# Moving the first pass's statistics, masks, normalising and residual add off VectorE onto ScalarE, TensorE and GpSimd

## The reference

```
x = x + L0(gn(x))      # a 2-D selective scan ("Mamba" block)
x = x + L1(gn(x))      # attention with 12 heads and relative positions

L0:  xh, z = split(x @ in_proj.T)                  # 192 channels each
     u = silu(depthwise_conv3x3(xh) + conv_b)
     four directions k (row and column order, each forward and backward):
       dt, B, C = split(x_proj[k] @ u)             # 24, 16, 16 rows
       dt = softplus(dt_proj[k] @ dt + dt_b[k])
       h[n] = h[n] * exp(dt * A[n]) + dt * u * B[n]    # over the tokens, n = 0..15
       y += sum_n h[n] * C[n] + D[k] * u
     y = layernorm(y) * g + b;  return (y * silu(z)) @ out_proj.T
```

## Time and profile before

| | |
|---|---|
| median of 3 runs | 3307.79 us (3305.24 to 3314.67) |
| the profiled execution | 3309.41 us, span 3307.6 us |
| TensorE busy | 2748.0 us (83% of the span) |
| VectorE busy | 2366.0 us (72%) |
| ScalarE busy | 1557.4 us (47%) |
| GpSimd busy | 1335.6 us (40%) |
| mean granted TensorE clock | 0.948 |

### The profile page before, as it was taken

How to read it: one execution, slowest core, us unless ns; L and a number is a source line. 1 busy time by engine, 2 the same in 40 slices (tenths; PEclk the granted TensorE clock), 3 DMA queues, 4 the chain that set the end, 5 groups by cost and what they waited for, 6 DMA issues and landing times. The chain is left out here.

```text
span 3307.6 us, 40573 instructions
## 1 busy us (share of the span) xinstructions
PE 2748.0 (83%) x15824; PEld 1382.7 (42%) x15824; DVE 2366.0 (72%) x2262; ACT 1557.4 (47%) x1908; POOL 1335.6 (40%) x636
## 2 busy tenths in 40 slices
PE   3577777887678876777667999989998999989999
PEld 1222223332233332222222665556554665555655
DVE  1598899999999999999982466625664356625665
ACT  4445644555435564444431356514563346514564
POOL 4478766887668876766651100011000200011000
PEclk8789998999999999999896999999999999999999
DMA  1334443355443544445541111020111110020110
GB/s 61 128 115 133 153 144 141 130 140 159 145 149 127 140 159 145 161 134 144 182 137 60 30 33 52 1 71 1 33 52 40 33 33 25 29 71 1 33 52 20
DMA packets 93429, 297.51 MB, mean 90 GB/s; under 512 B 15804, under 2 KB 18504, under 8 KB 93224
## 3 DMA queue, kind: packets, MB, share of 16 engines
q1 hardware_dynamic: 93224, 294.73, 28.6%
HBM read 238.57 MB, written 23.07 MB: 79 GB/s over the span
## 5 line engine op out<-in xcount | busy, mean ns | idle before, releaser
L1608 POOL TENSOR_TENSOR arena<-arena 128x1024 f32<-128x1024 f32 x384 | 902.9, 2365 | 325.9 <-DVE arena L1092 277.3
L1092 DVE TENSOR_TENSOR_SCAN arena<-PS,arena 128x1024 f32<-128x1024 f32 x384 | 878.2, 2287 | 86.1 <-ACT PS L1445 62.5
L1445 ACT ACTIVATE PS<-arena,a_inf,a_neg 128x1024 f32<-128x1024 f32 x384 | 463.8, 1208 | 776.8 <-DVE arena L1092 772.4
L564 PE MATMUL PS<-arena,ident 128*128 128x512 f32 x1568 | 804.1, 639 | 19.3 <-ACT arena L1456 15.1
L1225 DVE CUSTOM_DVE_ANT_1 arena<-PS,arena 128x1024 f32<-128x1024 f32 x384 | 467.6, 1219 | 350.4 <-PE PS L851 350.4
L1533 ACT ACTIVATE arena<-arena,neg_max 128x1024 f32<-128x1024 f32 x384 | 441.0, 1149 | 513.4 <-DVE neg_max L1225 513.4
L555 PE MATMUL PS<-arena,sel 96*128 96x512 bf16 x768 | 247.7, 406 | 413.0 <-DVE arena L1100 409.3
L1100 DVE TENSOR_TENSOR arena<-arena,PS 128x1024 f32<-128x1024 f32 x384 | 459.3, 1196 | 9.7 <-PE PS L555 8.9
L564 PEld LDWEIGHTS PS<-arena,ident 128*128 128x128 f32 x1568 | 318.5, 204 | 304.2 <-issue 246.9
L851 PE MATMUL PS<-arena 64*128 64x512 f32 x1536 | 433.1, 641 | 11.1 <-DMA arena<-arena 11.1
L862 PE MATMUL PS<-ident,arena 128*128 128x128 f32 x3072 | 413.9, 278 | 2.6 <-ACT arena L1533 2.6
(11 more groups left out here) (125 smaller groups left out, 2286.2 us busy)
## 6 DMA issues: line engine op xcount, KB each, us to landing
arena<-b_rows SPq DMA_DIRECT2D x256, 512.0 KB, 3.7
arena<-b_rows SPq DMA_DIRECT2D x256, 256.0 KB, 4.0
arena<-arena SPq DMA_DIRECT2D x192, 128.0 KB, 2.9
arena<-arena SPq DMA_DIRECT2D x120, 64.0 KB, 2.0
normed<-xn SPq DMA_DIRECT2D x5, 1536.0 KB, 6.4
normed<-x_in SPq DMA_DIRECT2D x4, 1536.0 KB, 7.9
residual<-x_in SPq DMA_DIRECT2D x4, 1536.0 KB, 8.0
x<-residual SPq DMA_DIRECT2D x4, 1536.0 KB, 6.4
```

The lines of the kernel that those rows point to most:

```text
L564: last = pe.matmul(dst[:, half(h)], lhs, rhs[:, half(h)], start=start, stop=stop, skip_group_check=True)
L1092: dve.tensor_tensor_scan(HS[:, at % 2, ::step], DA[:, ::step], DBU[:, at % R3, ::step], 0.0, ALU.mult, ALU.add).then_inc(scan_done.sem, 1)
L1445: act.activation(DA, DELTA[:, tile % 2, :], ACT.Exp, bias=a_inf[:, col:col + 1], scale=a_neg[:, col:col + 1]).then_inc(da_ready.sem, 1)
L1608: pool.tensor_tensor(DBU[:, at % R3, :], DU[:, tile % 2, :], BSB[:, at % R3, :], ALU.mult).then_inc(dbu_ready.sem, 1)
```

## The change

- **Statistics.** ScalarE makes the sums of both group norms: Copy and Square with an accumulator, over 1024 columns for the first norm, over the 512 of each output half for the second. It reads the group means from PSUM (`group_means`), GpSimd makes variance and bias, ScalarE rstd and the normalising (Identity with scale and bias).
- **x + out** is a third product, an identity times x, in TensorE's output product; ScalarE copies the sum out.
- **The mask** of the softplus is a Relu on ScalarE into uint8 (item 8); the scaling by 1/3 is folded into the square.
- **The split of C**: GpSimd subtracts (from a copy in SBUF), ScalarE casts.
- **Image 0's front**: its additions, caps and gates go from GpSimd to VectorE.
- **Positions**: a front's group norm moves to the end of the image before (negative positions; for image 1 squeezed into items 0 to 3), the tap additions are spaced otherwise, and many jobs stand elsewhere.

VectorE keeps scan, product with C, series and choice, and centring and scaling of the layernorm. The core of the diff:

```diff
+EARLY = 20
-PE_FRONT = {("stats",): 4, ("xh", 0): 12, ("xh", 1): 13, ("xh", 2): 14, ("pad", 0): 36, ("pad", 1): 37, ("pad", 2): 38,
+PE_FRONT = {("stats",): -8, ("xh", 0): 5, ("xh", 1): 6, ("xh", 2): 7, ("pad", 0): 25.5, ("pad", 1): 26, ("pad", 2): 27,
             ("z", 0, 0): 56, ("z", 0, 1): 57, ("z", 0, 2): 58, ("z", 1, 0): 61, ("z", 1, 1): 62, ("z", 1, 2): 63,
             ("dts", 0): 70, ("dts", 1): 71, ("dts", 2): 72, ("bc", 0): 75, ("bc", 1): 76, ("bc", 2): 77}
+PE_MID = {("y", 0, 0): 9, ("y", 0, 1): 10, ("y", 0, 2): 11, ("y", 1, 0): 13, ("y", 1, 1): 14, ("mean", 0): 21,
+          ("mean", 1): 22, ("var", 0): 30, ("var", 1): 31, ("out", 0): 43, ("out", 1): 44, ("out", 2): 45,
+          ("out", 3): 46, ("out", 4): 47, ("out", 5): 48, ("stats",): 53}
-ACT_FRONT = {("rstd",): 8, ("xh",): 16, ("pad",): 40, ("z", 0): 60, ("z", 1): 64.5,
...
+ACT_FRONT = {("stat", 0, 0): -20, ("stat", 0, 1): -19, ("stat", 1, 0): -18, ("stat", 1, 1): -15, ("stat", 2, 0): -14,
+             ("stat", 2, 1): -11, ("means",): -6, ("rstd",): -4, ("norm", 0): -3, ("norm", 1): -2, ("norm", 2): -1,
+             ("xh",): 8, ("pad",): 28, ("z", 0): 59.5, ("z", 1): 64.5,
+             ("sig", 0, 0): 35, ("sig", 0, 1): 38, ("sig", 0, 2): 40, ("sig", 1, 0): 62, ("sig", 1, 1): 65,
+             ("sig", 1, 2): 65.5, ("sig", 2, 0): 60, ("sig", 2, 1): 64, ("sig", 2, 2): 67.5, ("sig", 3, 0): 70,
+             ("sig", 3, 1): 74, ("sig", 3, 2): 75, ("ucopy", 0): 49.5, ("ucopy", 1): 50, ("ucopy", 2): 67,
+             ("ucopy", 3): 69, ("dts",): 73.5, ("brows",): 79, ("bchi",): 80, ("bmid",): 83, ("blo",): 86}
+ACT_MID = {("yf", 0): 12, ("yf", 1): 16, ("sq", 0): 27, ("sq", 1): 28.5, ("rstd",): 33, ("affine", 0): 35.5,
+           ("affine", 1): 37, ("out", 0): 43.9, ("out", 1): 44.9, ("out", 2): 45.9, ("out", 3): 46.9, ("out", 4): 47.9,
+           ("out", 5): 48.9, ("means",): 54.9, ("rstd2",): 56, ("norm", 0): 58.9, ("norm", 1): 60.5, ("norm", 2): 61}
+POOL_FRONT = {("var",): -5.5, ("bias",): -3.5, ("cap", 0): 36.5, ("u", 0): 42, ("cap", 2): 63, ("cap", 1): 64,
+              ("u", 1): 65.9, ("gate", 0): 68.5, ("cap", 3): 71.5, ("gate", 1): 77, ("rest", 0): 81.5, ("rest", 1): 85}
+POOL_MID = {("gate", 0): 38.5, ("gate", 1): 40, ("sums",): 50, ("var",): 55.5, ("bias",): 57}
...
-SP_FRONT = {("next_x",): 72, ("z_store",): 79, ("b_store",): 83, ("bcs",): 87}
+SP_FRONT = {("next_x",): 72, ("z_store",): 80, ("b_store",): 83, ("bcs",): 89}
...
+            if f == 1 and at < 0:
+                item = (at + EARLY) * 0.2
...
                     half_product(banks(k % 2, 1), h, [
                         (W["w_out"][:, 0, c * P:(c + 1) * P], flat(yf(m, 0))),
-                        (W["w_out"][0:XT, 1, c * P:(c + 1) * P], flat(yf(m, 1)[0:XT, :]))]).then_inc(op_psum.sem, 1)
+                        (W["w_out"][0:XT, 1, c * P:(c + 1) * P], flat(yf(m, 1)[0:XT, :])),
+                        (idn, flat(X[:, c, :]))]).then_inc(op_psum.sem, 1)
...
             def soft_series(tile):
 
-                dve.wait_ge(soft_e.sem, soft_e.at(tile + 1))
-                dve.tensor_scalar(MASK, SE, SMALL, None, ALU.is_lt)
                 dve.wait_ge(soft_q2.sem, soft_q2.at(tile + 1))
-                dve.scalar_tensor_tensor(out=SQ3, in0=SQ3, scalar=2.4375, in1=SE, op0=ALU.add,
+                dve.scalar_tensor_tensor(out=SQ3, in0=SQ3, scalar=0.8125, in1=SE, op0=ALU.add,
                                          op1=ALU.mult).then_inc(soft_q.sem, 1)
...
+                elif what == "out":
+                    k, = args
+                    h, c = divmod(k, CT)
+                    act.wait_ge(op_psum.sem, op_psum.at(2 * CT * m + k + 1))
+                    act.activation(X[:, c, half(h)], banks(k % 2, 1), ACT.Copy, accum_out=half_sums[:, h, c, 0:1])
+                    act.activation(banks(k % 2, 1), banks(k % 2, 1), ACT.Square, scale=1.0 / IMG,
+                                   accum_out=half_sums[:, h, c, 1:2]).then_inc(x_saved.sem, 1)
...
+            def small_mask(tile):
+
+                act.activation(MASK, SE, ACT.Relu, bias=mask_top[:, 0:1], scale=-MASK_TOP / SMALL
+                               ).then_inc(soft_mask.sem, 1)
```

More of the change, by code:

```diff
@@ L49 @@
[L49 to L53, removed]
@@ L73, in due @@
-def due(table, i):
-    return sorted((job for job, at in table.items() if i <= at < i + 1), key=table.get)
+            POOL_FRONT[("add", _m, _j)] = _b
+SIG_ORDER = sorted(range(4), key=lambda which: ACT_FRONT[("sig", which, 0)])
+SIG_DONE = sorted(range(4), key=lambda which: ACT_FRONT[("sig", which, 2)])
+CAP_ORDER = sorted(range(4), key=lambda which: POOL_FRONT[("cap", which)])
+SP_FRONT = {("next_x",): 72, ("z_store",): 80, ("b_store",): 83, ("bcs",): 89}
+SP_MID = {("x_load",): 1, ("z_load",): 2, ("x1_store",): 52, ("xn2_store",): 67}
@@ L78, in in_order, with front_due, mid_due @@
 def in_order(table):
     return sorted(table, key=table.get)
+def front_due(table, b, i):
+    found = []
+    for job, at in table.items():
+        for f in (b + 1, b + 2):
+            item = at + ITEMS * (f - b - 1)
+            if f == 1 and at < 0:
+                item = (at + EARLY) * 0.2
+            if f < B and i <= item < i + 1:
+                found.append((item, f, job))
+    return [(f, job) for item, f, job in sorted(found, key=lambda found: found[0])]
+def mid_due(table, b, i):
+    return sorted((job for job, at in table.items() if b and i <= at < i + 1), key=table.get)
@@ L251, in build @@
         xn_loaded = signal("xn_loaded", unit=16)
-        gn1_stats, gn1_psum, gn1_var, gn1_rstd = [signal(f"gn1_{k}") for k in ("stats", "psum", "var", "rstd")]
+        gn1_stats, gn1_psum, gn1_means, gn1_var, gn1_rstd, gn1_bias = [
+            signal(f"gn1_{k}") for k in ("stats", "psum", "means", "var", "rstd", "bias")]
         xn_normed = signal("xn_normed")
@@ L975, in _ @@
             dve.wait_ge(prep.sem, PREPARED_BY - 1)
-            link_a = steps(dve, dve_a)
-            def stats(r, src, k, h):
-                return dve.bn_stats(bn[r][:, k, h, :], src[:, k, half(h)])
-            def group_moments(r, done):
-                for k in range(CT):
-                    last = dve.bn_aggr(mv[r][:, k, :], bn[r][:, k, :, :])
-                link_a(last)
-                link_a(dve.tensor_tensor(g_tmp[r][:, :], mv[r][:, :, 0], mv[r][:, :, 0], ALU.mult))
-                dve.tensor_tensor(mv[r][:, :, 1], mv[r][:, :, 1], g_tmp[r][:, :], ALU.add).then_inc(done.sem, 1)
@@ L1101, in times_c @@
                                   ).then_inc(hc_ready.sem, 1)
-            for job in in_order(DVE_FRONT):
-                front(0, *job)
+            for job in in_order(POOL_FRONT):
+                if job[0] not in ("var", "bias"):
+                    front_products(dve, 0, *job)
             dve.wait_ge(consts.sem, consts.at(N_CONST))
@@ new lines, in mid @@
+            def mid(m, what, *args):
+                if what == "gate":
+                    j, = args
+                    rows = (P, XT)[j]
+                    if j == 0:
+                        pool.wait_ge(z_loaded.sem, z_loaded.at(2 * m + 2))
+                    pool.wait_ge(ya_ready.sem, ya_ready.at(2 * m + j + 1))
+                    pool.tensor_tensor(yf(m, j)[0:rows, :], yf(m, j)[0:rows, :], zs(m, j)[0:rows, :], ALU.mult
+                                       ).then_inc(yg_ready.sem, 1)
+                elif what == "sums":
+                    pool.wait_ge(x_saved.sem, x_saved.at(2 * CT * (m + 1)))
+                    pool.tensor_tensor(mv[1][:, :, :], half_sums[:, 0, :, :], half_sums[:, 1, :, :], ALU.add
+                                       ).then_inc(gn2_stats.sem, 1)
+                elif what == "var":
+                    pool.wait_ge(gn2_means.sem, gn2_means.at(m + 1))
+                    group_variance(1, gn2_var)
+                else:
+                    pool.wait_ge(gn2_rstd.sem, gn2_rstd.at(m + 1))
+                    pool.tensor_tensor(g_bias[1][:, :], gs[1][:, 0, :], g_rstd[1][:, :], ALU.mult).then_inc(gn2_bias.sem, 1)
```

398 lines of the change are left out of this document (189 added, 209 removed).

## The result

The change makes the kernel slower: 3445.07 us median (3443.72 to 3447.86) against 3308.34 us (3305.24 to 3314.67) in the same runs, a ratio of 1.0412 [1.0395, 1.0428]. The prediction was 3453 us, with 3385 to 3530 as its range. The profiled execution has a span of 3443.4 us, a mean granted clock of 0.932, and 2265.9 us of busy VectorE, 100 us less than before. **VectorE was relieved as planned, and the time went up by 137 us.**

The account below looks back on a forecast made before the run. It took a loop of VectorE's scan and ScalarE's decay, 3.57 us per item, as the bound. Scan stage 236 - 99 = +137 us, before the scans -4, after them +12: 3453 us against the median, range 3385 to 3530.

Parts of the forecast that it names:

- The bound, and the place of TensorE in an item: Scan stage: scan and ScalarE's decay alternate, 3.57 us per item; TensorE's item runs one item later than ScalarE's.
- Output products in the same item, 170 us: Items 43 to 48, three images: ScalarE waits for TensorE's product, 11.3 then 13.4 us per item, 57 us per image.
- rival 2: Output items: the clock stays at 1.2 GHz, 16.6 us per item, 65 us more, 3518 us; chance 0.15.
- One item apart, 45.4 and 4.5 us for u: Scan stage: ScalarE's savings one item after TensorE's product wait, 45.4 us; GpSimd's gating of u part 1 adds 4.5.
- The price of the earlier trace: Second z product, items 63 to 64: scan 2.7 us later than usual, 3.2 us after three product items in a row.
- The series keeps the mask's wait, 41 us: Softplus in the scans: the series inherits the mask's 1.78 us wait for GpSimd, 23 times, so 41 us stay.
- rival 3: Softplus in the scans: the series is not blocked, 34 of the 41 us are gained, 3419 us; chance 0.13.
- Gain of 99 us: Scan stage: net gain from work leaving VectorE, 158 - 41 - 16 - 8 + 6 us.
- Image 1's first items, 10.6 us: Items 0 to 3: image 1's squeezed front costs 10.6 us, 5.4 of it for means in TensorE's own item 2.
- Before the scans -4: Before the first scan: VectorE taking image 0's additions saves 10 us, statistics and normalising on ScalarE give 6 back.
- After the scans +12: Behind the last scan: half as many more output products at a granted clock of 0.50 cost 12 us.
- Rival 1: Whole kernel: freed VectorE decides, TensorE is ready when ScalarE asks, waits are not paid, 3215 us; chance 0.09.

Follow-up runs that it names:

- out_filler: Kernel after the change, with six more constant products on TensorE behind each of the first five output products of images inside the scans; 3412.87 us, ratio 1.0303.
- others_alone: Kernel after the change, output products left in the same item, ScalarE's other savings moved one item later; 3382.03 us, ratio 1.0212.
- mask_alone: Kernel before the change, with only the softplus mask moved from VectorE to ScalarE (Relu into uint8 at item 8); 3302.25 us, ratio 0.997.

## Why the prediction was right, and where it was off

- **The bound, and the place of TensorE in an item** (from the earlier trace rows): right, and it carries everything. A wait of ScalarE delays the next scan by its whole length.
- **Output products in the same item, 170 us**: measured 170.4. The cycles of image 2 were 11.19, 12.93, 13.29, 13.47, 13.57 and 13.61 us; 11.3 and then 13.4 were predicted. The low end of the ring, 11.2, is shown by out_filler, and rival 2 (clock low throughout, 16.6 us) is out: from the third turn on the clock rises during the output product. The close fit of the whole is partly luck, since the second cycle was still shorter and the last were longer, and since the terms of the turn shown above differ both ways: saving 1.19 us for 1.45, C product and accumulation 4.24 for 4.11, output product 3.35 for 3.0 (part of it at the low clock); added up, the prediction's own terms give 13.3, not 13.4. Two of its signs don't fit its own sum: it had ScalarE wait 5 to 9 us for each output, where a ring of 13.4 us leaves 10.7 and the trace has 194.5 / 18 = 10.8; and it had scans wait "some 200 us" for ScalarE, where 62.5 + 170 + 45 make 278 and 299.5 came.
- **One item apart, 45.4 and 4.5 us for u**: others_alone takes 60.3 us away. Some 8 of these (2.7 us at item 64, three times) are in the kernel before already, so about 52 were added where the prediction had 49.9. The sum is near, its terms are not: y part 0 12.6 for 9.6, y part 1 6.9 and a larger wait at z part 1 (4.4 to 4.9 for 2.7) not thought of, means up to 10.0 for 5.4, z part 0 some 6.0 for 9.6, and the dts, charged with 9.6, cost nothing: item 73 has no excess in any image, for item 72, 3.5 us longer than 3.57 by its blocked series, lets TensorE catch up, and its last dts product ends 1.1 us behind the start of item 73's scan. The price of the earlier trace rows was used everywhere, but it depends on how late TensorE is when the item begins.
- **The series keeps the mask's wait, 41 us**: right in kind. mask_alone shows it, and rival 3 is out. In the kernel after the series takes 64.0 us for 24, 35 more than at 1.21 each; in mask_alone the mask's items were 0.6 us shorter each, where 0.69 were assumed. VectorE as a whole is 100 us less busy, where 115 were forecast.
- **Gain of 99 us**: some 7 less, if the small costs are taken as predicted. Of the 381.1 us, 60.3 and 170.4 go to the waits above; 150.4 remain. The prediction's terms leave 233.8 - 8 (z part 1, which is among the 60.3) - 99 + 16.2 (its small costs: 10.6, 2.6 and 3) = 143.0. In single items most of what was thought to come, came: 3.4 at items 9 to 11 (normalising), 3.0 at 60 to 63, 4.7 at 80 to 87 (the split) in image 2, and the returned wait of TensorE behind the pair's saving at items 2 to 4. Which of the smaller items lack the 7 us I did not isolate.
- **Image 1's first items, 10.6 us**: they hold 10.9, 7.5 more than before. The total is luck: item 2, with the means in TensorE's own item, holds 8.6 for a predicted 5.4, and items 0, 1 and 3 together 2.3 for 5.2.
- **Before the scans -4**: the first scan starts 3.5 us earlier; over all traces it starts at 115.8 to 119.9 us with the change and at 122.8 and 123.3 without.
- **After the scans +12**: wrong, -8. The step that failed is the clock: I took 0.50 for 36 matmuls from 24 that ran at 0.50, and they took 24.3 us instead of 36. That is 12 of the 20 us; the other 8 lie behind the products, 2 up to the attention and 6 in it, where the prediction had nothing, and part of them is chance. The other end that the prediction named, -5, is near -8 by luck: it stood for a clock that rises and shortens the products, and they took as long as the kernel before's. Scan stage +147.3 instead of +137 and this term cancel: 10 too little and 20 too much, which is why the total is 8 us off and looks better than its parts.
- **Rival 1** (VectorE decides, 3215 us) was put at 0.09 for this kernel, rightly; but its condition, that TensorE is ready when ScalarE asks, is what the experiments made: two items in the tables gave 3237 us, and the spread outputs with the store moved 3223. The relief of VectorE was worth nearly what rival 1 said; the tables withheld it. Not all of the 87 us below the kernel before are that relief: some 8 come from z part 1, which waited there too, and a few from before the first scan and behind the last.

## What to carry to other kernels

When work moves from one engine to another, look at where the new owner stands in its own program when the input is ready: an engine that waits inside an item passes its wait to all that is behind it, and the same 18 jobs cost 170 us or, two items further apart, 31 us. Before a term is multiplied, ask whether the late engine's next job depends on the delay: if not, it is paid once. And if a result is made later, follow every queue that waits for it, the one that issues loads above all: a store ahead of its data held back the rows of B and cost 6.8 us per image.

## What the runs showed of the hardware

- The granted clock rose from 0.50 half-way through 36 gapless matmuls in 24.3 us (output products with the identity product as third part), and stayed at 0.50 through 24 gapless ones of two parts (24.11 and 24.10 us in two kernels). TensorE was busy all the time in each stretch.
- In a ring with 5.92 us of idle TensorE per turn, the C product and accumulation ran at the low level (1.03 and 3.62 us) and the output's last part at the high one (1.12 for two), and so in the turns beside it. Twelve extra matmul records in the idle time (5.31 us) held the clock at 1.00 and made the turn 2.2 us shorter on the mean.
- On ScalarE each accumulator is read by an instruction of its own, 186 to 194 ns on the mean. These reads overlapped the passes: from the first pass of an output saving to the decay behind it went 1.19 us (1209.64 to 1210.83), as long as the two passes of 0.60 and 0.59.
- A VectorE instruction with two SBUF inputs took over the wait for GpSimd when the one ahead of it was removed: 2.56 us for 1.21, and 4.71 where two GpSimd instructions followed each other.
- A store that waited 15.1 us for its data in SyncE's queue held back the loads issued behind it: the first row of B was issued at 1101.19, behind the store, and GpSimd had its row at 1109.66.
